# Issuing the activation loads ahead of the weight loads, and the q reload ahead of the x reload

## The chip, the cores and the metric

The kernel runs on the 8 cores of one Trainium2 chip, one core for each of the 8 sequences of the batch. The cores exchange nothing. The metric is the device time of the slowest core, in microseconds.

## The reference

One transformer layer, for x of 8 x 4096 x 1024:

```python
x = x + attn(layernorm(x), w_qkv, w_proj, b_proj)
x = x + ffn(layernorm(x), w1, b1, w2, b2)

def attn(x, ...):                 # 16 heads of 64, linear attention
    q, k, v = split(x @ w_qkv.T)
    q, k = relu(q), relu(k)
    ksum = k.sum(over the sequence)
    z = 1 / (ksum . q + eps)
    context = v k^T               # per head, summed over the whole sequence
    return (context q * z) @ w_proj.T + b_proj

def ffn(x, ...):
    return relu(x @ w1 + b1) @ w2 + b2        # 1024 -> 4096 -> 1024
```

The context sums over the whole sequence, so attention's output needs all of k and v first. The kernel therefore has two stages.

## The kernel before

Activations are held transposed, 1024 channels as 8 chunks of 128 partitions, tokens along the free dimension. TensorE computes in bf16.

**Stage A** (lines 130 to 370) goes over 8 tiles of 512 tokens. For each tile: the load `xa` (f32 in HBM, cast to bf16 by the transfer, 1 MB written, two buffers); VectorE's squares (line 224); TensorE's column sums of x and of its squares against a vector of ones, `emit_statsA` (lines 234 and 239); mean and rstd on VectorE and ScalarE; their broadcast by TensorE (lines 293 and 297); the normalized tile `lnx` on VectorE (lines 307 and 310). Then the q projection (line 277), whose results ScalarE evicts to `qout` (line 285, two buffers) and SP stores to the HBM scratch `qsc` (line 287, 64 stores of 128 KB); then the k and v projection (line 332); then the context (line 184).

The loop is software pipelined and runs from i = 0 to 8. TensorE's program order is: i = 0: statistics of tile 0, broadcast 0, statistics of tile 1. i = 1: Q of tile 0, broadcast 1, K and V of tile 0, context of tile 0, statistics of tile 2. i = 2: Q of tile 1, broadcast 2, and so on. So the statistics of tile i + 1 always stand ahead of Q of tile i. VectorE's order in a step is LayerNorm of tile i, squares of tile i + 1, accumulation of the context of tile i - 1.

The tiles from 2 on are loaded by line 217: in step i GpSimd waits until LayerNorm of tile i - 1 has read its buffer, and issues the load of tile i + 1 into it.

Three engines issue transfers, each on its own queue. GpSimd's queue carries all transfers that cast: `wqkv_sb` (6 MB written, line 164), W1 (8 MB, line 165, in the trace `w_sb`), the projection weights (2 MB, line 166), eight casts of W2 from HBM to HBM as bf16 (`w2bf`, 1 MB each, line 168), and the `xa` tiles (lines 211, 212, 217). All of these but line 217's are issued without a wait, in the order of their lines. SP's queue carries the `qsc` stores.

**Stage B** (line 371 on), behind a barrier of all engines, goes over 16 tiles of 256 tokens: q is reloaded as `qb` (0.5 MB, two buffers), multiplied by the sums of k (`emit_zden`, line 454) and by the context (line 535), scaled by z, projected (line 603), added to the reloaded f32 x (`x1`, 1 MB, two buffers, line 630), normalized, and sent through the two FFN products (lines 673 and 707). W1 is resident, W2 is streamed from `w2bf`. The small table `zsel_sb` is loaded at the start of stage B on GpSimd's queue (line 403) and used by line 551. The first two `x1` and the first two `qb` are issued at lines 465 and 468, by SP, once all `qsc` stores have landed.

Of the kernel before, what the change touches and what calls it, by code (L numbers as in the profile page):

```python
# [18 lines left out]
NB_A = 512  # L19
# [22 lines left out]
def WG(eng, sem, v):  # L42
    if v > 0:
        sem.maxwait = max(sem.maxwait, v)
        eng.wait_ge(sem.h, v)


def build_nc():
    nc = bass.Bass("TRN2", target_bir_lowering=False)
# [14 lines left out]
    xT_r = xT.ap().rearrange("(c p) n -> p c n", p=128)  # L64
# [3 lines left out]
    qsc_r = qsc.ap().rearrange("(c p) n -> p c n", p=128)  # L68
# [3 lines left out]
    with st:  # L72
# [15 lines left out]
        s_xa = [S("s_xa0"), S("s_xa1")]  # L88
# [8 lines left out]
        s_qb = [S(f"s_qb{r}") for r in range(2)]  # L97
# [28 lines left out]
        with ExitStack() as sta:  # L126
# [4 lines left out]
            xa = SA("xa", [128, 2, CK, NB_A], BF16)  # L131
# [29 lines left out]
                kvt[:, :, 1024:2056].rearrange("p s (pr x) -> p s pr x", x=129)[:, :, :, 128:129],  # L161
                1.0))

            s_wq.inc(nc.gpsimd.dma_start(wqkv_sb[:, :, :], wqkvT_r), 16)
            s_w1.inc(nc.gpsimd.dma_start(w1_sb[:, :, :], w1_r), 16)
            s_wp.inc(nc.gpsimd.dma_start(wproj_sb[:, :, :], wprojT_r), 16)
            for d in range(CK):
# [40 lines left out]

            for i in range(NBA + 1):
                if i == 0:  # L210
                    s_xa[0].inc(nc.gpsimd.dma_start(xa[:, 0, :, :], xT_r[:, :, 0:NB_A]), 16)
                    s_xa[1].inc(nc.gpsimd.dma_start(xa[:, 1, :, :], xT_r[:, :, NB_A:2 * NB_A]), 16)
                elif i + 1 < NBA:
                    WG(nc.gpsimd, s_pa1, 8 * i)
                    WG(nc.gpsimd, s_sqp, 8 * i)

                    s_xa[(i + 1) % 2].inc(nc.gpsimd.dma_start(
                        xa[:, (i + 1) % 2, :, :], xT_r[:, :, (i + 1) * NB_A:(i + 2) * NB_A]), 16)
# [154 lines left out]
        with ExitStack() as stb:  # L373
            SBB = lambda name, shape, dt: stb.enter_context(nc.sbuf_tensor(name, shape, dt))
            projtmp = SBB("projtmp", [128, CK, NB_B], F32)
            qb = SBB("qb", [128, 2, CK, NB_B], BF16)
# [30 lines left out]
            NB = NB_B  # L407
# [51 lines left out]
            for b in range(NBB + 1):  # L459
                if b == 0:  # L460
                    s_mz2.inc(nc.scalar.memzero(PB[7][32:33, 0:NB]))
                    WG(nc.sync, s_qst[0], 16 * (4 * NBA))
                    WG(nc.sync, s_qst[1], 16 * (4 * NBA))
                    for t in range(2):
                        s_xb[t].inc(nc.sync.dma_start(
                            x1[:, t, :, :], xT_r[:, :, t * NB:(t + 1) * NB]), 16)
                    for t in range(2):
                        s_qb[t].inc(nc.sync.dma_start(
                            qb[:, t, :, :], qsc_r[:, :, t * NB:(t + 1) * NB]), 16)
                else:  # L470
                    if b + 1 < NBB:
                        t = b + 1
                        WG(nc.sync, s_mmattn, 8 * b)
                        WG(nc.sync, s_qst[0], 16 * 4 * (t // 2 + 1))
                        WG(nc.sync, s_qst[1], 16 * 4 * (t // 2 + 1))
                        s_qb[t % 2].inc(nc.sync.dma_start(
                            qb[:, t % 2, :, :], qsc_r[:, :, t * NB:(t + 1) * NB]), 16)
# [243 lines left out]
                if b >= 1 and b + 1 < NBB:  # L721
                    t = b + 1
# [56 lines left out]
```

How the kernel before makes its waits and increments, by code:

```python
    def inc(self, inst, k=1):  # L36
        inst.then_inc(self.h, k)
        self.n += k
        return self.n
# [2 lines left out]
def WG(eng, sem, v):  # L42
    if v > 0:
        sem.maxwait = max(sem.maxwait, v)
        eng.wait_ge(sem.h, v)
```

## Time and profile before

| | us |
|---|---|
| median of 2 runs | 1875.01 (1869.11 to 1880.91) |
| the profiled execution | 1873.58 |
| its span (slowest core, core 5) | 1872.5 |
| spans of the eight cores | 1852.5 to 1872.5 |
| TensorE busy in the span | 1583.6 (85%) |
| VectorE busy | 603.0 (32%) |
| ScalarE busy | 486.2 (26%) |
| GpSimd busy | 117.5 (6%) |

The profile is of one execution, read on its slowest core; times within it count from the first instruction. The trace has 12000 matmuls. A row of a timeline shows start, duration, engine, line, operation, output and input, count, and in brackets the idle time of the engine before it with what ended it. "SPq" and "POOLq" are the queues on which SP and GpSimd issue transfers; a landing time counts from the issue.

### The profile page before, as it was taken

How to read it: one execution, taken by the hardware profiler on the slowest of the kernel's cores; microseconds unless marked ns; L12 is line 12 of the kernel's file. 1: busy time of each engine (PE TensorE's matmuls, PEld its weight loads, DVE VectorE, ACT ScalarE, POOL GpSimd, SP SyncE). 2: the span in 40 equal slices, each digit the busy share in tenths (PEclk: the TensorE clock that was granted, in tenths of full speed). 3: DMA queues.
4: the chain of work that ended last, by engine and by line, in shares of the span. 5: the costliest groups of instructions: out<-in, count | busy, mean ns of one | idle time of the engine just before them, and what ended most of it. 6: DMA issues, size and time to landing. Idle time of an engine off the chain costs nothing.

```text
span 1872.5 us, 32607 instructions; the slowest of 8 cores (1852.5 to 1872.5 us)
## 1 busy us (share of the span) xinstructions
PE 1583.6 (85%) x12000; PEld 1118.9 (60%) x12000; DVE 603.0 (32%) x1295; ACT 486.2 (26%) x1033; POOL 117.5 (6%) x218
## 2 busy tenths in 40 slices
PE   0000599999999559999999999999999999999998
PEld 0000144344444227887887777877878778788787
DVE  0000433343332154334333342342333433433400
ACT  0000123223323114224133142241331422422421
POOL 1000000000000001101011011010110110110100
PEclk9999799999999869999999999999999999999999
DMA  9999412211200211534534336245343362453353
GB/s 150 163 133 106 61 37 46 46 27 42 46 23 23 67 58 46 194 134 147 188 124 163 126 127 216 96 147 186 121 167 124 120 231 91 147 191 136 135 203 113
DMA packets 90007, 220.25 MB, mean 118 GB/s; under 512 B 4592, under 2 KB 70128, under 8 KB 72192
## 3 DMA queue, kind: packets, MB, share of 16 engines
q0 software_dynamic: 21072, 100.70, 22.4%
q1 hardware_dynamic: 68784, 117.48, 18.4%
q8 instruction: 102, 1.67, 0.4%
q14 instruction: 49, 0.40, 0.1%
HBM read 226.58 MB, written 33.55 MB: 139 GB/s over the span
## 4 chain that ended last, share of the span: by engine, by line
PE 61%; ACT 1%; issue 1%; DVE 1%; DMA 1%; SPq 0%; DVEq 0%; ACTq 0%
PE PB L707 24%; PE PB L673 23%; PE PB L603 7%; PE PB L535 2%; PE PB L551 2%; PE PB L553 1%; PE PB L454 1%; PE PB L512 1%; PE PB L507 1%; ACT hT L683 1%; DMA qb<-qsc 1%; ACT msq L421 0%; ACT PB L649 0%; PE PB L579 0%; DVE zrow L442 0%
## 5 line engine op out<-in xcount | busy, mean ns | idle before, releaser
L673 PE MATMUL PB<-ln,w_sb 128*128 128x256 bf16 x4096 | 459.5, 272 | 9.8 <-ACT hT L683 9.3
L707 PE MATMUL PB<-hT,w2t 128*128 128x256 bf16 x4096 | 449.7, 273 | 2.9 <-ACT hT L683 2.1
L707 PEld LDWEIGHTS PB<-hT,w2t 128*128 128x128 bf16 x4096 | 399.6, 98 | 53.0 <-issue 6.9
L673 PEld LDWEIGHTS PB<-ln,w_sb 128*128 128x128 bf16 x4096 | 370.3, 97 | 93.4 <-issue 17.9
L683 ACT ACTIVATE hT<-PB,b1c_sb 128x256 bf16<-128x256 f32 x512 | 241.4, 474 | 269.5 <-PE PB L673 268.6
L332 PE MATMUL PAkv<-wqkv_sb,lnx 128*128 128x512 bf16 x1024 | 225.2, 382 | 0.0
L715 DVE SCALAR_TENSOR_TENSOR outb<-PB,b2c_sb,x 128x256 f32<-128x256 f32 x128 | 61.9, 483 | 383.9 <-PE PB L707 383.9
L234 PE MATMUL PAst<-xa,ones 128*1 128x512 bf16 x64 | 18.5, 441 | 192.1 <-DMA xa<-xT 192.1
L332 PEld LDWEIGHTS PAkv<-wqkv_sb,lnx 128*128 128x128 bf16 x1024 | 100.3, 99 | 127.1 <-issue 9.5
L565 ACT ACTIVATE zbcs<-PB 128x256 f32<-128x256 f32 x128 | 49.1, 384 | 461.2 <-PE PB L553 453.3
L603 PE MATMUL PB<-attnT,wproj_sb 128*128 128x256 bf16 x1024 | 142.0, 308 | 1.0 <-DVE attnT L571 0.5
L277 PE MATMUL PAq<-lnx,wqkv_sb 128*128 128x512 bf16 x512 | 118.2, 391 | 15.5 <-ACT qout L285 15.5
L603 PEld LDWEIGHTS PB<-attnT,wproj_sb 128*128 128x128 bf16 x1024 | 110.7, 111 | 30.2 <-issue 3.8
L234 PEld LDWEIGHTS PAst<-xa,ones 128*1 128x1 bf16 x64 | 5.3, 91 | 201.9 <-issue 196.6
L277 PEld LDWEIGHTS PAq<-lnx,wqkv_sb 128*128 128x128 bf16 x512 | 50.2, 100 | 82.9 <-issue 29.2
L494 POOL CAST xbf<-x 128x256 bf16<-128x256 f32 x128 | 68.9, 584 | 461.3 <-DVE x L630 461.3
L630 DVE SCALAR_TENSOR_TENSOR x<-projtmp,bprojc_sb,x 128x256 f32<-128x256 f32 x128 | 53.6, 479 | 98.9 <-DMA x<-xT 62.9
L224 DVE TENSOR_TENSOR xsqA<-xa 128x512 bf16<-128x512 bf16 x64 | 22.1, 418 | 189.7 <-DMA xa<-xT 189.7
L307 DVE TENSOR_TENSOR tmpA<-xa,PAq 128x512 f32<-128x512 bf16 x64 | 44.0, 687 | 108.2 <-PE PAq L297 101.9
L259 ACT ACTIVATE msqA<-varA 1x512 f32<-1x512 f32 x8 | 5.0, 628 | 269.3 <-DVE varA L256 269.3
L484 POOL DMA_DIRECT2D w2t<-w2bf x64 | 33.7, 529 | 646.5 <-PE PB L707 646.5
L610 ACT ACTIVATE projtmp<-PB 128x256 f32<-128x256 f32 x128 | 49.2, 384 | 96.5 <-PE PB L603 86.8
(92 smaller groups left out, 925.3 us busy)
## 6 DMA issues: line engine op xcount, KB each, us to landing
w2t<-w2bf SPq DMA_DIRECT2D x64, 1024.0 KB, 7.2
w2t<-w2bf POOLq DMA_DIRECT2D x64, 1024.0 KB, 5.6
x<-xT SPq DMA_DIRECT2D x16, 1024.0 KB, 10.1
outT<-outb SPq DMA_DIRECT2D x16, 1024.0 KB, 5.4
w_sb<-w POOLq DMA_DIRECT2D x1, 8192.0 KB, 92.9
w2bf<-w2r POOLq DMA_DIRECT2D x8, 1024.0 KB, 144.4
xa<-xT POOLq DMA_DIRECT2D x8, 1024.0 KB, 9.0
qsc<-qout SPq DMA_DIRECT2D x64, 128.0 KB, 1.8
```

Source lines behind the costliest of these rows:

```text
L277: q_mm = nc.tensor.matmul(PAq[j % 2][:, 0:NB_A], wqkv_sb[:, c, j * 128:(j + 1) * 128], lnx[:, ii % 2, c, :], start=(c == 0), stop=(c == CK ...
L307: s_pa1.inc(nc.vector.tensor_tensor(tmp[:, :], xa[:, i % 2, c, :], PAq[0][:, 0:NB_A], ALU.mult))
L332: kv_mm = nc.tensor.matmul(PAkv[bank][:, 0:NB_A], lnx[:, ii % 2, c, s * 128:(s + 1) * 128], wqkv_sb[:, c, C + jt * 512:C + (jt + 1) * 512] ...
L494: s_cast2.inc(nc.gpsimd.tensor_copy(xbf2[:, c, :], x1[:, b2 % 2, c, :]))
L565: s_qz.inc(nc.scalar.activation(zbcs[:, p % 2, :], PB[ZBANK[p % 3]][:, 0:NB], AF.Copy))
L603: pj_mm = nc.tensor.matmul(PB[6 + j % 2][:, 0:NB], wproj_sb[:, d, j * 128:(j + 1) * 128], attnT[:, d, :], start=(d == 0), stop=(d == CK - 1))
L610: s_pev.inc(nc.scalar.activation(projtmp[:, j, :], PB[6 + j % 2][:, 0:NB], AF.Copy))
L630: s_x1.inc(nc.vector.scalar_tensor_tensor(x1[:, b2 % 2, k, :], projtmp[:, k, :], bprojc[:, k:k + 1], x1[:, b2 % 2, k, :], ALU.add, ALU.add))
L673: f1_mm = nc.tensor.matmul(PB[w % 2][:, 0:NB], w1_sb[:, c, w * 128:(w + 1) * 128], ln2[:, bb % 2, c, :], start=(c == 0), stop=(c == CK - 1))
L683: s_hev.inc(nc.scalar.activation(hT[:, w, :], PB[w % 2][:, 0:NB], AF.Relu, bias=b1c[:, w:w + 1]))
L707: f2_mm = nc.tensor.matmul(PB[2 + d % 2][:, 0:NB], w2t[:, d % 4, w, :], hT[:, w, :], start=(w == 0), stop=(w == WK - 1))
L715: s_oev.inc(nc.vector.scalar_tensor_tensor(outb[:, d, :], PB[2 + d % 2][:, 0:NB], b2c[:, d:d + 1], x1[:, bb % 2, d, :], ALU.add, ALU.add))
```

## The change

The two first `xa` loads, issued by GpSimd at the head of the loop behind all weight loads, are issued among them: tile 0 ahead of `wqkv_sb`, tile 1 between `wqkv_sb` and W1. At the start of stage B, SP issues the two `qb` loads ahead of the two `x1` loads. No transfer is added or taken away, and no wait is changed.

```diff
@@ -161,7 +161,9 @@
+            s_xa[0].inc(nc.gpsimd.dma_start(xa[:, 0, :, :], xT_r[:, :, 0:NB_A]), 16)
             s_wq.inc(nc.gpsimd.dma_start(wqkv_sb[:, :, :], wqkvT_r), 16)
+            s_xa[1].inc(nc.gpsimd.dma_start(xa[:, 1, :, :], xT_r[:, :, NB_A:2 * NB_A]), 16)
             s_w1.inc(nc.gpsimd.dma_start(w1_sb[:, :, :], w1_r), 16)
             s_wp.inc(nc.gpsimd.dma_start(wproj_sb[:, :, :], wprojT_r), 16)
             for d in range(CK):
@@ -208,8 +210,7 @@
             for i in range(NBA + 1):
                 if i == 0:
-                    s_xa[0].inc(nc.gpsimd.dma_start(xa[:, 0, :, :], xT_r[:, :, 0:NB_A]), 16)
-                    s_xa[1].inc(nc.gpsimd.dma_start(xa[:, 1, :, :], xT_r[:, :, NB_A:2 * NB_A]), 16)
+                    pass
                 elif i + 1 < NBA:
@@ -462,11 +463,11 @@
                     for t in range(2):
+                        s_qb[t].inc(nc.sync.dma_start(
+                            qb[:, t, :, :], qsc_r[:, :, t * NB:(t + 1) * NB]), 16)
+                    for t in range(2):
                         s_xb[t].inc(nc.sync.dma_start(
                             x1[:, t, :, :], xT_r[:, :, t * NB:(t + 1) * NB]), 16)
-                    for t in range(2):
-                        s_qb[t].inc(nc.sync.dma_start(
-                            qb[:, t, :, :], qsc_r[:, :, t * NB:(t + 1) * NB]), 16)
```

## Rows read from the trace of the kernel before

**Rows 1.** The page's 40 slices: TensorE and DMA busy, in tenths of each slice.

```profile
PE   0000599999999559999999999999999999999998
DMA  9999412211200211534534336245343362453353
```

**Rows 2.** Waits until 720 us: engine and line, releaser, total, times, longest.

```profile
PE PAst L234 <- DMA xa<-xT: 192.1, 1, 192.1
...
PE PB L454 <- DMA qb<-qsc: 19.5, 1, 19.5
```

**Rows 3.** Timeline of GpSimd at the start: start, duration, what it issues.

```profile
1.57 1.04 POOL L164 DMA_DIRECT2D wqkv_sb<-wqkvT  x1 [0.87 <-POOLq L49]
2.61 0.89 POOL L165 DMA_DIRECT2D w_sb<-w  x1
...
8.26 0.99 POOL L211 DMA_DIRECT2D xa<-xT  x1
9.18 0.96 POOL L212 DMA_DIRECT2D xa<-xT  x1
```

**Rows 4.** Views of lines 168, 211 and 212, in this order: issue to landing.

```profile
DMA to landing us min/median/max: 113.2/144.4/175.8
...
DMA to landing us min/median/max: 183.7/183.7/183.7
...
DMA to landing us min/median/max: 188.7/188.7/188.7
```

**Rows 5.** DMA view until 198 us: transfer, queue, count, KB each, us to landing.

```profile
w_sb<-w POOLq DMA_DIRECT2D x1, 8192.0 KB, 92.9
...
wqkv_sb<-wqkvT POOLq DMA_DIRECT2D x1, 6144.0 KB, 42.5
```

**Rows 6.** Timeline of TensorE: statistics of tile 0, Q of tiles 0 and 1.

```profile
192.12 2.29 PE L234 MATMUL PAst<-xa,ones 128*1 128x512 bf16 x5 [192.12 <-DMA xa<-xT]
...
195.45 1.91 PE L239 MATMUL PAst<-xsqA,ones 128*1 128x512 bf16 x4
...
222.19 3.63 PE L277 MATMUL PAq<-lnx,wqkv_sb 128*128 128x512 bf16 x16
...
276.25 3.63 PE L277 MATMUL PAq<-lnx,wqkv_sb 128*128 128x512 bf16 x16
282.15 12.21 PE L277 MATMUL PAq<-lnx,wqkv_sb 128*128 128x512 bf16 x48 [2.28 <-ACT qout L285]
```

**Rows 7.** Window: length, busy of PE, PEld, DVE, ACT, POOL, clock, DMA share, GB/s.

```profile
206.00:219.00 13.00, 3.35 (x9) 0.85 (x7) 11.42 (x18) 0.00 (x0) 0.76 (x1) 0.50 0.00 1
```

**Rows 8.** View of line 217, the six later `xa` loads: issue to landing.

```profile
DMA to landing us min/median/max: 8.2/8.4/11.0
```

**Rows 9.** View of line 287, the 64 `qsc` stores: issue to landing.

```profile
DMA to landing us min/median/max: 1.8/1.8/3.9
```

**Rows 10.** The page's queues: SP's, with packets, MB, share of 16 engines.

```profile
q1 hardware_dynamic: 68784, 117.48, 18.4%
```

**Rows 11.** Timeline of the start of stage B.

```profile
643.98 1.01 SPq L465 DMA_DIRECT2D x<-xT  x2
645.04 4.78 SPq L468 DMA_DIRECT2D qb<-qsc  x2
...
654.82 1.86 PE L454 MATMUL PB<-qb,ksmat 128*16 128x256 bf16 x8 [19.54 <-DMA qb<-qsc]
...
667.32 0.36 SPq L476 DMA_DIRECT2D qb<-qsc  x1
...
669.57 0.48 DVE L630 SCALAR_TENSOR_TENSOR x<-projtmp,bprojc_sb,x 128x256 f32<-128x256 f32 x1 [1.76 <-ACT projtmp L610]
```

**Rows 12.** Views of line 465, and of line 476 from 660 to 690 us: landing.

```profile
DMA to landing us min/median/max: 6.3/7.3/8.4
...
DMA to landing us min/median/max: 4.0/4.0/4.0
```

**Rows 13.** DMA view from 630 to 720 us: the `zsel_sb` load.

```profile
zsel_sb<-zsel POOLq DMA_DIRECT2D x1, 32.0 KB, 5.7
```

## The prediction

> **What bounds the kernel now.** I read the page's slices first. TensorE is idle in the first four of the 40 slices and busy in nearly all the others, while the DMA engines are full in just those four [rows 1]. The table of waits then names two long waits of TensorE on a transfer: 192.1 us at line 234, the first statistics of stage A, for the `xa` load; and 19.5 us at line 454, the start of stage B, for the `qb` load [rows 2]. Both are on the path that sets the end, because TensorE is the busy engine behind each of them. The change touches exactly these two places and nothing else.
>
> Why 192 us for a tile of 1 MB: the timeline of the start shows that GpSimd issues `wqkv_sb` at 1.57, `w_sb` (W1) at 2.61, after it the projection weights and the eight `w2bf` casts (lines 166 and 168), and only then, at 8.26 and 9.18, the two `xa` tiles [rows 3]. Their landing times, counted from the issue, are 183.7 and 188.7 us, so they arrive at 192.0 and 197.9 [rows 4]. The landings come in the order of the issues: `wqkv_sb` at 1.6 + 42.5 = 44.1, W1 at 2.6 + 92.9 = 95.5, the `w2bf` casts spread from 113.2 to 175.8 after their issues, then `xa` [rows 3 to 5]. The DMA engines are full all the while [rows 1]. So this queue works first in, first out, at the full rate of the DMA engines, and what matters for a load is what is queued ahead of it.
>
> **Part 1, the order on GpSimd's queue.** No transfer is added or removed. `xa` tile 0 goes ahead of `wqkv_sb`, tile 1 behind it, ahead of W1.
>
> Cost of 1 MB (written) in the full queue: W1 is 8 MB in 95.5 - 44.1 = 51.4 us, 6.4 us each; the second `xa` came 5.9 us after the first. I take 6.0 to 6.2 for an `xa`.
>
> New arrivals: `xa` 0 is first, issued near 1.6, at the 8.4 us (median) of such a load later in the kernel [rows 8]: 10. `wqkv_sb`: 44.1 + 6.2 = 50.3. `xa` 1: 56.5. Tile 0's LayerNorm is long done by then. TensorE's program order is statistics(0), broadcast(0), statistics(1), Q(0), so Q(0) waits for `xa` 1 too. Statistics of a tile that has just landed took from 192.12 to 195.45 + 1.91 = 197.4, 5.2 us [rows 6]. Q(0) therefore starts at 56.5 + 5.2 = 61.7; before, it was 222.19 [rows 6]. Seen there, 160 us are gained. They don't last.
>
> The next thing that is late is tile 2. Its load (line 217) is issued by GpSimd when tile 0's LayerNorm has freed the buffer, at the latest near 10 + 30 = 40 us (from 192.12 to Q(0) at 222.19 was 30) [rows 6]. It joins the same queue, behind W1, the projection weights and all eight casts. And TensorE's order puts statistics(2) ahead of Q(1), so nothing of tile 1 beyond its LayerNorm can be computed until `xa` 2 is there. Tile 0 keeps TensorE from 61.7 for 276.25 - 222.19 = 54.1 us [rows 6], to about 116. Then TensorE stands again.
>
> Arrival of `xa` 2: the queue ahead of it is the same set of transfers as was ahead of the end at 197.9, in another order. One more tile: 197.9 + 6.0 = 203.9. New on these engines is that tile 0's eight `qsc` stores now run inside the full stretch. The hardware queue moved 117.48 MB in 18.4% of the span [rows 10], 344.5 us, 2.9 us per MB; the stores are 1 MB: +3. Take 207, bounds 204 (the stores fit in gaps) and 221. The far bound: the load of 1 MB that ran beside compute landed in 8.2 to 11.0 us [rows 8]; if all loads in the 54 us of tile 0 ran slower by 11.0 / 8.2 = 1.34, the queue loses 54 x (1 - 1/1.34) = 14 us. I choose near the lower end, since a lone load's time includes its own start, which a queue filled well ahead hides.
>
> Q(1) then starts at 207 + 5.2 = 212; before, 276.25. That is 64 us, and from there on the program is the same one. One cost comes with it: TensorE restarts Q(1) straight out of an idle stretch. After the 192 us idle its granted clock was 0.50 (the 1.2 GHz level) from 206 to 219 [rows 7]; only Q(0), 30 us after the first statistics, ran its first 16 matmuls in 3.63 us as Q(1) did [rows 6]. With 16 matmuls of Q(1) at half speed the 3.6 us become about 7, of which the 2.28 us wait behind them, for ScalarE, hides most [rows 6]. I take 2, between 0 (all hidden) and 5 (half speed over twice that stretch). Gain of part 1: 64 - 2 = 62 us, bounds 45 and 67.
>
> Issue costs: 1 us of GpSimd's issue ahead of `wqkv_sb` is inside the 6.2. Tile 3's load (line 217 at the next step) waits for tile 1's LayerNorm only, near 97, so it follows `xa` 2 by 6 us, long before TensorE needs it. W1 lands 12 us later than before, at 108, needed only in stage B; the casts end near 196, needed in stage B too. These are free, by hundreds of microseconds.
>
> Tile 0's Q phase itself will be slower than the 18 us that Q(1) had (276.25 to 282.15 + 12.21) [rows 6]: ScalarE's eviction j waits for the store of j - 2, and a store landed in 1.8 us, in 3.9 at most [rows 9]. It has 207 - 116 = 91 us of slack, so this costs nothing.
>
> **Part 2, the order on SP's queue at stage B.** Before, two `x1` tiles of 1 MB are issued at 643.98, then two `qb` of 0.5 MB at 645.04; TensorE starts line 454 at 654.82 [rows 11]. Now `qb` 0 goes first, at 643.98. The nearest row for a `qb` issued into an idle queue with 2 MB of loads right behind it is the one at 667.32: 4.0 us to landing [rows 11, 12]. So line 454 starts at 648.1: 6.7 us. Bounds: 1 MB of `x1` issued first took 6.3 us [rows 12], so at least 4.4; a 128 KB store's 1.8 [rows 9] would give at most 8.9. The Trainium skill, "DMA: Bandwidth & Descriptors", section "Anatomy of one DMA — SWDGE (gpsimd) path", fits a DMA as 2.0 us plus bytes at 436 GB/s, for the other kind of queue; as an estimate 3.2 us here, by which this gain would be 7.5 instead of 6.7. The row is longer, and the row stands in the sum.
>
> What is late next: `x1` 0, now behind 1 MB of `qb`. It is wanted by VectorE at line 630, 669.57 before [rows 11], about 662.9 after. Two MB from an idle start landed in 8.4 + 0.4 us (`x1` 1) [rows 12], so `x1` 0 is there at 653; 10 us to spare. `zsel_sb`, on GpSimd's queue, landed 5.7 us after its issue, at 650, beside the same 3 MB [rows 13]; it is wanted only after line 454's 1.86 us and VectorE's work on them, past 650. Uncovered, either would cost back at most the 6.7.
>
> **Sum.** 62 + 6.7 = 69 us. Against the profiled execution (1873.58 us, span 1872.5) that is 1804.9; its time is 1.4 below the median of the runs, 1875.01. I predict 1805. By the bounds of the terms the sum is 49 to 76, that is 1798 to 1824.
>
> **The rivals.**
> (a) The gain of the start stays whole: `xa` 2 gets past the queued weights (its own share of the engines) and lands before 116. Then Q(0)'s 160 us hold, with 6.7: 1707. Against it: the first two tiles, issued by 9.2, landed behind everything issued before them [rows 3, 4]. 3%.
> (b) Compute slows the full queue by the far bound, 14 us instead of 3: Q(1) at 221 + 5.2 = 226, 50 us gained, less 2 for the restart, and 6.7: 1873.6 - 54.7 = 1819. For it only the 11.0 us landing [rows 8]. 8%.
> (c) Part 2 gives nothing, because `x1` or `zsel_sb` becomes the wait: 1812. Against it the 10 us of slack. 4%.
> (d) Slower than before: the `qsc` stores starve behind the full load queue. Q(0) holds three store round trips in a row, L each. Tile 0 ends at 61.7 + 3L + 36 (the 54.1 less its Q phase of 18). It reaches `xa` 2 from L = 36. It eats the whole gain when it ends at 276 + 7 = 283, which is L = 62; at L = 75 it ends at 323, 40 us later, and the kernel takes 1914. Against it: L was 3.9 us at most [rows 9]. The Trainium skill, same page, section "Queues, rings and completion order", has each DMA engine take turns between queues at packet granularity, which by itself would keep L within a few packets; the 3.9 us agrees, though no store ran beside a queue this deep. 2%.
> (e) The change does little: the queue before `xa` 2 is stretched by 33 us or more (8 us per MB instead of 6.4 over the 20 MB behind `xa` 1). Then 1838 to 1870. The rates of the queue, 6.4 us per MB for W1, were even. 2%.
>
> **How the numbers follow.** The forecast has 81%. Its own range is 1798 to 1812; before's two runs lie 6 us either side of their median, which widens it to 1793 to 1818. Range with (b) and (c): 1793 to 1821. About 2% (37 us, below 1837.5) is what a measurement of this kernel can tell from no change. Faster by more: the forecast, (a), (b), (c), 96%. Within: 2%. Slower by more: 2%.
>
> **What the profile would show.** Waits: TensorE at line 234 twice, once for about 10 us at the start, once for 80 to 95 us ending near 207, plus a wait for `xa` 1 or `wqkv_sb` ending near 56; Q(0) near 61, Q(1) near 212. Landing of the first line-217 load near 170 us. Line 454 first starts 4 to 5 us after the first `qb` issue. I am wrong if Q(1) starts much before 205 (not first in, first out) or after 225 (queue slowed), or if line 630 waits for `x1` at the first block.

## The result, and the profile after

The changed kernel takes 1808.3 us (median of 11 runs) against 1873.3 before (10 runs). The ratio is 0.965, with a 95% interval of 0.963 to 0.967: 66 us, or 3.5%, faster. (Here and below a few runs, in which one half of the chip ran slower, stand in the medians but not in the ratios; where the two differ, the ratio counts.) The forecast was 1805, with a range of 1793 to 1821. The profiled execution took 1800.57 us, its slowest core is core 0 with a span of 1799.5.

The page's slices of the changed kernel, in tenths, one slice 45 us; they answer to [rows 1]:

```profile
PE   1364299999997599999999999999999999999998
PEclk7667599999999689999999999999999999999999
DMA  9999722112000314352463534634436255363463
```

TensorE now has work in the first slices, but little of it, and at a lower granted clock: of the first four slices, idle before, none is more than six tenths busy, and the fifth holds two tenths. The waits until 660 us (engine and line, releaser, total, times, longest) say why; they answer to [rows 2]:

```profile
PE PAst L235 <- DMA xa<-xT: 108.4, 3, 58.5
...
ACT qout L286 <- DMA qsc<-qout: 44.5, 7, 11.4
...
PE PB L455 <- DMA qb<-qsc: 15.2, 1, 15.2
```

The wait of 192.1 us has become three, together 108.4, the longest 58.5. The wait at stage B went from 19.5 to 15.2. The second row has grown: ScalarE waits for the `qsc` stores, 44.5 us in seven waits, where it was 9.7 us in four before. The timeline of TensorE (start, duration, line; it answers to [rows 6]) puts them in order:

```profile
62.41 2.29 PE L235 MATMUL PAst<-xa,ones 128*1 128x512 bf16 x5 [31.39 <-DMA xa<-xT]
...
66.69 3.63 PE L278 MATMUL PAq<-lnx,wqkv_sb 128*128 128x512 bf16 x16
72.50 5.30 PE L278 MATMUL PAq<-lnx,wqkv_sb 128*128 128x512 bf16 x16 [2.18 <-ACT qout L286]
85.00 3.57 PE L278 MATMUL PAq<-lnx,wqkv_sb 128*128 128x512 bf16 x8 [7.21 <-ACT qout L286]
...
153.20 1.98 PE L186 MATMUL PActx<-kvt 128*128 128x129 bf16 x32 [1.21 <-ACT kvt L348]
213.64 2.29 PE L235 MATMUL PAst<-xa,ones 128*1 128x512 bf16 x5 [58.46 <-DMA xa<-xT]
...
218.82 3.85 PE L278 MATMUL PAq<-lnx,wqkv_sb 128*128 128x512 bf16 x16
224.72 10.52 PE L278 MATMUL PAq<-lnx,wqkv_sb 128*128 128x512 bf16 x48 [2.05 <-ACT qout L286]
```

Q(0) starts at 66.7 instead of 222.2, tile 0 is done at 155, and then TensorE waits 58 us until tile 2 lands at 213.6. Q(1), which was at 276.25 on the slowest core before, is at 218.8. The view of the store line (288) from 60 to 130 us shows how tile 0's eight stores fared beside the full queue (time from issue to landing); before, 3.9 us was the longest [rows 9]:

```profile
DMA to landing us min/median/max: 9.9/15.1/58.2
```

Stage B, which answers to [rows 11]:

```profile
582.52 1.00 SPq L466 DMA_DIRECT2D qb<-qsc  x2
583.58 5.12 SPq L469 DMA_DIRECT2D x<-xT  x2
...
589.02 1.86 PE L455 MATMUL PB<-qb,ksmat 128*16 128x256 bf16 x8 [15.19 <-DMA qb<-qsc]
...
603.77 0.48 DVE L631 SCALAR_TENSOR_TENSOR x<-projtmp,bprojc_sb,x 128x256 f32<-128x256 f32 x1 [1.76 <-ACT projtmp L611]
```

Line 455 starts 6.5 us after SP's first issue instead of 10.8, and line 631 waits for ScalarE as before, not for `x1`.

Where the 66 us are, as a mean over the eight cores' timelines: Q(1) starts at 216.8 (215.2 to 219.0) instead of 273.0 (270.5 to 276.3), 56 us; from the last context product to the first product of stage B 15.9 instead of 21.6 us, 6 us. Together 62. Another 1.6 us lie between Q(1) and the last context product (353.5 instead of 355.1). The rest lies in stage B; neither is in a step that the change touches, and no run explains it.

### The profile page after: what moved, and what is told of

The parts are those of the page before. It is cut to its first block, busy times and chain, and to the rows that moved or that the text cites. A ratio compares the mean times of both kernels' runs of the same rounds, so it can differ in the third digit from the quotient of the medians.

```text
span 1799.5 us, 32607 instructions; the slowest of 8 cores (1786.8 to 1799.5 us)
## 1 busy us (share of the span) xinstructions
PE 1583.6 (88%) x12000; PEld 1116.1 (62%) x12000; DVE 603.3 (34%) x1295; ACT 486.2 (27%) x1033; POOL 117.6 (7%) x218
## 4 chain that ended last, share of the span: by engine, by line
PE 63%; ACT 1%; issue 1%; DVE 1%; DMA 0%; DVEq 0%; ACTq 0%; SPq 0%
PE PB L708 25%; PE PB L674 24%; PE PB L604 7%; PE PB L536 2%; PE PB L552 2%; PE PB L554 1%; PE PB L513 1%; PE PB L455 1%; PE PB L508 1%; ACT hT L684 1%; DMA qb<-qsc 0%; ACT msq L422 0%; ACT PB L650 0%; PE PB L580 0%; DVE zrow L443 0%
## 5 line engine op out<-in xcount | busy, mean ns | idle before, releaser
L278 PE MATMUL PAq<-lnx,wqkv_sb 128*128 128x512 bf16 x512 | 125.5, 407 | 35.3 <-ACT qout L286 35.3
L604 PE MATMUL PB<-attnT,wproj_sb 128*128 128x256 bf16 x1024 | 135.6, 298 | 1.3 <-DVE attnT L572 0.7
L604 PEld LDWEIGHTS PB<-attnT,wproj_sb 128*128 128x128 bf16 x1024 | 106.3, 106 | 28.3 <-issue 4.4
L235 PE MATMUL PAst<-xa,ones 128*1 128x512 bf16 x64 | 19.8, 465 | 108.4 <-DMA xa<-xT 108.4
L619 DVE TENSOR_TENSOR tmp<-x,PB 128x256 f32<-128x256 f32 x128 | 53.9, 421 | 59.0 <-PE PB L586 47.3
L498 DVE TENSOR_TENSOR xsq<-x 128x256 bf16<-128x256 f32 x128 | 65.2, 575 | 2.7 <-DVE x L631 2.6
```

The source lines that it names most:

```text
L278: q_mm = nc.tensor.matmul(PAq[j % 2][:, 0:NB_A], wqkv_sb[:, c, j * 128:(j + 1) * 128], lnx[:, ii % 2, c, :], start=(c == 0), stop=(c == CK ...
L498: s_sq2p.inc(nc.vector.tensor_tensor(xsq2[:, c, :], x1[:, b2 % 2, c, :], x1[:, b2 % 2, c, :], ALU.mult))
L604: pj_mm = nc.tensor.matmul(PB[6 + j % 2][:, 0:NB], wproj_sb[:, d, j * 128:(j + 1) * 128], attnT[:, d, :], start=(d == 0), stop=(d == CK - 1))
L619: s_pa2.inc(nc.vector.tensor_tensor(tmp2[:, :], x1[:, bb % 2, k, :], PB[4][:, 0:NB], ALU.mult))
```

## Experiments

### Each part alone

Part 1 alone puts the two `x1` loads back ahead of `qb`:

```diff
                     for t in range(2):
-                        s_qb[t].inc(nc.sync.dma_start(
-                            qb[:, t, :, :], qsc_r[:, :, t * NB:(t + 1) * NB]), 16)
-                    for t in range(2):
                         s_xb[t].inc(nc.sync.dma_start(
                             x1[:, t, :, :], xT_r[:, :, t * NB:(t + 1) * NB]), 16)
+                    for t in range(2):
+                        s_qb[t].inc(nc.sync.dma_start(
+                            qb[:, t, :, :], qsc_r[:, :, t * NB:(t + 1) * NB]), 16)
```

> Only the first part of the change: the two first activation loads ahead among the weights; stage B issues x1 ahead of qb as before. Theory (the two parts add, and nearly all of the gain is in the first one): the changed kernel's time plus what the qb order gives, 4 to 7 us, so 1812 to 1816; line 454 starts about 10.8 us after SP's first issue of stage B instead of 6.5. Rival (the order in stage B gives nothing, because x1 becomes the wait at the first block): the same time as the changed kernel, about 1808.

Measured: ratio 0.967 (0.965 to 0.970), some 5 us above the changed kernel, the two intervals overlapping. From the last context product to the first product of stage B its cores take 22.6 us, against 15.9.

Part 2 alone is the opposite edit, on the kernel before.

> Only the second part: stage B issues qb ahead of x1, the start of stage A is as before. Theory: 4 to 7 us faster than before, 1866 to 1870, with the first qb landing in 4 to 6.5 us. Rival (x1 or zsel late): no change, 1873.

Measured: ratio 0.994 (0.992 to 0.997), 1868.7 us, 11 us below its own runs of before (7 to 15). Its trace shows the same 15.9 us at that place as the changed kernel has, so 6 us are located and the rest of the 11 isn't. No sign of the rival. The parts add: 0.0326 + 0.0058 is 0.0384 where 0.0351 was measured for both, within their intervals.

### Do the slow stores of tile 0 cost anything?

Six `qout` buffers instead of two (four unused rows of stage A are dropped to make room):

```diff
-            qout = SA("qout", [128, 2, NB_A], BF16)
+            qout = SA("qout", [128, 6, NB_A], BF16)
...
-                        WG(nc.scalar, s_qst[j % 2], 16 * (kq // 2))
+                        WG(nc.scalar, s_qst[kq % 6], 16 * (kq // 6))
```

> The changed kernel with six qout buffers instead of two, so that the eviction of a q block waits for the store of six blocks before. In the changed kernel tile 0's Q phase takes 50 us, because each store takes 10 to 15 us beside the full load queue. Theory (tile 0 has slack, tile 2's load sets Q(1)): tile 0's Q phase falls to 18 to 25 us, the wait for tile 2 grows by as much, Q(1) starts at the same time within 3 us, and the time stays at 1808 within 5. Rival (the slow stores reach the end): the time falls by about 30 us to 1778.

Measured: ratio 0.964 (0.962 to 0.966), the same as the changed kernel's 0.965. Its timeline of TensorE:

```profile
67.62 3.63 PE L274 MATMUL PAq<-lnx,wqkv_sb 128*128 128x512 bf16 x15
73.42 11.99 PE L274 MATMUL PAq<-lnx,wqkv_sb 128*128 128x512 bf16 x47 [2.18 <-ACT qout L282]
...
129.31 1.98 PE L182 MATMUL PActx<-kvt 128*128 128x129 bf16 x32 [1.21 <-ACT kvt L344]
218.06 2.29 PE L231 MATMUL PAst<-xa,ones 128*1 128x512 bf16 x5 [86.77 <-DMA xa<-xT]
```

The Q phase takes 18 us, tile 0 is done 24 us earlier, and the wait for tile 2 grew from 58 to 87 us. The stall was real and cost nothing: tile 2's load is what Q(1) hangs on. On the mean of the cores tile 2 is there at 214.7 us, 3 us later than with two buffers (211.8).

The stores taken out of the full stretch; tile 0's are made up for in the next tile's Q phase (so q of tile 0 is not the reference's). The counts that ScalarE waits for change with it:

```diff
-                        WG(nc.sync, s_qev, 8 * ii + j + 1)
-                        s_qst[j % 2].inc(nc.sync.dma_start(
-                            qsc_r[:, j, ii * NB_A:(ii + 1) * NB_A], qout[:, j % 2, :]), 16)
+                        if ii > 0:
+                            WG(nc.sync, s_qev, 8 * ii + j + 1)
+                            for jj in ([0, 1] if ii == 1 else [ii]):
+                                s_qst[j % 2].inc(nc.sync.dma_start(
+                                    qsc_r[:, j, jj * NB_A:(jj + 1) * NB_A], qout[:, j % 2, :]), 16)
```

> The changed kernel without the eight qsc stores of tile 0 while the loads run: in the next tile's Q phase each block is stored twice, to the columns of tiles 0 and 1, so q of tile 0 is not what the reference has. Same bytes, after the full stretch. Theory (the stores hold the engines 3 us, and everything else in the queue is what it was): tile 2's load lands 3 to 7 us earlier than in the changed kernel (there 210 to 214 over the cores), Q(0) takes 18 us. Rival (TensorE, VectorE and ScalarE at work slow the loads, the stores do not): tile 2 lands at the same time within 1 us, though Q(0) takes 18 us.

Measured in its trace: tile 2 is there at 208.2 us on the mean of the cores (205.6 to 209.7), against 211.8 (210.0 to 214.3) with the stores. On the slowest core:

```profile
67.25 3.87 PE L278 MATMUL PAq<-lnx,wqkv_sb 128*128 128x512 bf16 x16
73.06 10.52 PE L278 MATMUL PAq<-lnx,wqkv_sb 128*128 128x512 bf16 x48 [1.94 <-ACT qout L287]
...
209.56 2.29 PE L235 MATMUL PAst<-xa,ones 128*1 128x512 bf16 x5 [92.02 <-DMA xa<-xT]
```

So the eight stores cost the load queue 3.6 us, where the sum had 3, and the 208 that remain are the queue's own. This price depends on when the stores run: with six buffers, where they run closer together, tile 2 came 6.5 us later than without stores.

### What stands ahead of tile 2

The eight casts issued behind tile 2's load:

```diff
-            for d in range(CK):
+            def emit_cast(d):
                 s_w2pc.inc(nc.gpsimd.dma_start(
                     w2bf.ap()[d * 128:(d + 1) * 128, :, :],
                     w2r_h.ap()[d * 128:(d + 1) * 128, :, :]), 16)
...
                     s_xa[(i + 1) % 2].inc(nc.gpsimd.dma_start(
                         xa[:, (i + 1) % 2, :, :], xT_r[:, :, (i + 1) * NB_A:(i + 2) * NB_A]), 16)
+                    if i == 1:
+                        for d in range(CK):
+                            emit_cast(d)
```

> The changed kernel with the eight w2bf casts issued behind the load of tile 2 instead of ahead of it. Theory (what is queued ahead of tile 2 sets Q(1)): tile 2 lands when the projection weights have, near 140, tile 0 still ends near 153 because of its slow stores, so Q(1) starts near 158 instead of 212 to 219. Now Q(1) runs beside the casts, and its stores are slow too (10 to 15 us each, about 25 us more in the phase): Q(2) near 238 instead of 266 to 271, 30 us gained, 1778. Rival (the wait for tile 2 is not what the path hangs on; the total is set by the engines having to move all 27 MB first): Q(2) stays at 266 to 271 and the time at 1808.

Measured: ratio 0.960 (0.957 to 0.963), 1796.7 us: 10 us gained, not 30. The first half of the theory holds, the second was far too small:

```profile
154.82 3.63 PE L281 MATMUL PAq<-lnx,wqkv_sb 128*128 128x512 bf16 x16
160.73 5.30 PE L281 MATMUL PAq<-lnx,wqkv_sb 128*128 128x512 bf16 x16 [2.28 <-ACT qout L289]
196.61 3.57 PE L281 MATMUL PAq<-lnx,wqkv_sb 128*128 128x512 bf16 x8 [30.58 <-ACT qout L289]
215.64 5.40 PE L281 MATMUL PAq<-lnx,wqkv_sb 128*128 128x512 bf16 x16 [15.46 <-ACT qout L289]
...
260.47 3.63 PE L281 MATMUL PAq<-lnx,wqkv_sb 128*128 128x512 bf16 x16
```

Q(1) starts at 154.8 without a wait for tile 2, so what is queued ahead of it did set Q(1), and it moved by 60 us. But then TensorE stalls for 30.6 and 15.5 us inside Q(1), and Q(2) is at 260.5 where 238 was expected. The view of its store line, for the stores issued from 60 to 100 us (beside W1) and from 150 to 175 (beside the casts):

```profile
DMA to landing us min/median/max: 12.3/14.7/20.0
...
DMA to landing us min/median/max: 35.1/44.4/53.7
```

The second stretch holds only two stores. Beside the casts they took three times as long as those beside W1.

The same with six buffers:

> As the kernel before this one, with six qout buffers. Theory: the stores no longer hold tile 0 (it ends near 129) nor tile 1, so Q(1) starts near 145 when tile 2 has landed, and then tile 3's load, queued behind the casts and landing near 220, is the next wait: Q(2) near 226, 40 to 45 us gained on the changed kernel, about 1766. Rival (two buffers are enough here as they were in the run with six buffers alone): the same time as with two buffers.

Measured: ratio 0.957 (0.954 to 0.960), Q(1) at 146.7, Q(2) at 252.5 instead of 226. 15 us gained on the changed kernel instead of 40 to 45. The theory's next wait, for tile 3, did not come: it landed at 222, as said, while TensorE was in the K and V products. Before them TensorE had stood twice 24 us, at the end of Q(1), for ScalarE, which waited for the stores:

```profile
188.62 2.04 PE L293 MATMUL PAq<-m2A,ones1f 1*128 1x512 f32 x2 [23.79 <-ACT qout L285]
214.88 2.04 PE L297 MATMUL PAq<-varA,ones1f 1*128 1x512 f32 x2 [24.22 <-ACT qout L285]
```

All weights spread over the tiles, two buffers and then six:

```diff
+                    if i == 1:
+                        s_w1.inc(nc.gpsimd.dma_start(w1_sb[:, :, :], w1_r), 16)
+                    elif i == 2:
+                        s_wp.inc(nc.gpsimd.dma_start(wproj_sb[:, :, :], wprojT_r), 16)
+                        for d in range(3):
+                            emit_cast(d)
+                    elif i == 3:
+                        for d in range(3, CK):
+                            emit_cast(d)
```

> The changed kernel with W1 issued behind tile 2, the projection weights and three casts behind tile 3, five casts behind tile 4; two qout buffers. Theory (no activation load waits in the queue any more, but two buffers make every Q phase beside a full queue 20 to 30 us longer): Q(1) near 156, when tile 0 is done, Q(2) near 230, Q(3) near 295 instead of 317 to 324: 1775 to 1782. Rival (the store waits are hidden as before): Q(1) near 118, Q(3) near 225, 1710.

> The same with six qout buffers. Theory: Q(0) at 62 to 67, Q(1) near 130, Q(2) near 186, Q(3) near 240, no wait for an activation tile after the second: 80 to 88 us below the changed kernel, 1720 to 1728. Rival (six buffers can't keep up with 51 us of stores per tile, so that the stores hold each Q phase beside a full queue anyway): 1750 to 1775.

Measured: 0.961 (0.958 to 0.965) with two buffers: Q(1) and Q(2) came as said (160 and 232 on the mean of the cores), Q(3) at 314.7 on the slowest core did not, no better than the casts simply behind tile 2; 0.946 (0.939 to 0.952), 1768.4 us, with six. Its rival's range, not the theory's: with no activation tile late any more (Q(1) at 128.8), Q(2) came only at 206.9 and Q(3) at 278.7. Q(1) and Q(2) still ran beside casts; that this is the cause is what the next runs test.

### Casts and stores kept apart

Six buffers, W1 behind tile 2 and the projection weights behind tile 3 as in the two kernels before, and two casts at a time, each pair issued once a tile's q blocks are done (here the casts' part of the edit):

```diff
                 elif i + 1 < NBA:
+                    if i >= 3:
+                        WG(nc.gpsimd, s_mmkv, 16 * (i - 2) + 1)
+                        emit_cast(2 * (i - 3))
+                        emit_cast(2 * (i - 3) + 1)
                     WG(nc.gpsimd, s_pa1, 8 * i)
```

> Six qout buffers, W1 behind tile 2, the projection weights behind tile 3, and the eight w2bf casts two at a time, each pair issued when a tile's q blocks are done (during its K and V products, tiles 1 to 4), so that casts and qsc stores do not run together. Theory (the casts hold up the stores, 35 to 54 us for one store against 12 to 20 beside W1, and that is what the two spread kernels before this lost): Q phases of all tiles 18 to 25 us, Q(1) near 125 to 130, Q(2) near 180, Q(3) near 233 instead of 279: 45 us below the spread kernel with six buffers, about 1723. Rival (any load beside the stores holds them, W1 as much as the casts; or the casts spill over into the next tile's stores): 1745 to 1768.

Measured: ratio 0.916 (0.912 to 0.920), 1716 us by the ratio (lowest run 1716.0). Its timeline of TensorE, the first row of the Q phases of tiles 1, 2 and 3:

```profile
131.20 3.63 PE L280 MATMUL PAq<-lnx,wqkv_sb 128*128 128x512 bf16 x16
...
184.60 3.63 PE L280 MATMUL PAq<-lnx,wqkv_sb 128*128 128x512 bf16 x16
...
238.03 3.63 PE L280 MATMUL PAq<-lnx,wqkv_sb 128*128 128x512 bf16 x16
```

Every tile from 1 on takes 53 us, as before the change, and the stores issued from 130 to 300 us land in 2.0 us (median). The same bytes move on the same engines; only their timing against the stores differs.

The load of `wqkv_sb` cut in two, its q part ahead of tile 1 and its k and v part behind (TensorE waits for the second part before the first K and V product):

```diff
-            s_wq.inc(nc.gpsimd.dma_start(wqkv_sb[:, :, :], wqkvT_r), 16)
+            s_wq.inc(nc.gpsimd.dma_start(wqkv_sb[:, :, 0:C], wqkvT_r[:, :, 0:C]), 16)
             s_xa[1].inc(nc.gpsimd.dma_start(xa[:, 1, :, :], xT_r[:, :, NB_A:2 * NB_A]), 16)
+            s_wkv.inc(nc.gpsimd.dma_start(wqkv_sb[:, :, C:3 * C], wqkvT_r[:, :, C:3 * C]), 16)
```

> The same with the load of wqkv_sb in two: the q part (2 MB) ahead of tile 1, the k and v part (4 MB) behind it. Theory (Q(0) waits for 10 MB of queue, of which 4 MB are not needed yet): tile 1 lands near 38, Q(0) starts near 44 instead of 62 to 67, and the K and V products find their weights, there at 60 to 65: 18 us below the kernel without the split, about 1705. Rival (LayerNorm of tile 0, done near 43, or the K and V weights are late next): 5 us or less gained.

Measured: 1701.9 us, ratio 0.906 (0.902 to 0.910), 19 us below the kernel without the split, as said. Q(0) is at 45.3 and Q(1) at 99.3:

```profile
45.28 4.56 PE L281 MATMUL PAq<-lnx,wqkv_sb 128*128 128x512 bf16 x16
...
99.33 3.63 PE L281 MATMUL PAq<-lnx,wqkv_sb 128*128 128x512 bf16 x16
```

On the mean of the cores Q(1) came 30 us earlier than without the split (99.7 instead of 129.8), Q(2) only 19 (163.8 instead of 182.6): Q(1) now runs beside W1, and ScalarE waits 10 to 12 us for its stores there. The page's slices:

```profile
PE   2979999999956999999999999999999999999998
DMA  9999644500041353463525446352433626244263
```

This is the fastest of the kernels here, 106 us below the changed one. TensorE is at work from the second slice on, while the DMA engines are full for four slices as before.

The same with two buffers:

> The same as the split kernel with two qout buffers. Theory (a store beside a SBUF load takes 12 to 15 us, and with two buffers that is the pace of Q(0) and Q(1), beside the weights and W1, now without slack): Q(0) takes about 45 to 50 us instead of 20, Q(1) half that more: 35 to 50 us above the kernel with six buffers, 1740 to 1755. Rival (two buffers are enough once the casts are out of the way): within 5 us of it.

Measured: 1731.8 us, ratio 0.922 (0.918 to 0.926), 30 us more; Q(1) is at 138.6 instead of 99.3. The direction is the theory's, the size a little under it: Q(0) took 43 us, about as said, but Q(1) 18, no longer than elsewhere, since W1 had landed by then (at 122). The same buffers that were worth nothing in the changed kernel are worth 30 us here.

### Why the casts hold the stores

The DMA view of the queues (packets, MB, share of 16 engines) in stretches in which stores were under way. First the changed kernel from 67 to 117 us, beside W1; then the casts behind tile 2 with two buffers, from 162 to 195 us:

```profile
q0 software_dynamic: 1317, 7.65, 96.0%
q1 hardware_dynamic: 860, 0.78, 5.9%
```

```profile
q0 software_dynamic: 163, 3.64, 98.8%
q1 hardware_dynamic: 141, 0.13, 1.4%
```

Beside W1 GpSimd's queue passes 1317 packets in 50 us on 16 engines, 0.6 us each; beside the casts 163 in 33 us, 3.2 us each. The stores' queue passes nearly as many packets as the casts' (141 to 163). One store is 128 rows, 8 to an engine: at one row for each turn, 8 x 3.2 = 26 us, 52 for two under way (measured 35 and 54); beside W1 8 x 0.6 x 2 = 10 (measured 12 to 20). This is the Trainium skill's rule that each engine takes turns between its queues packet by packet ("DMA: Bandwidth & Descriptors", section "Queues, rings and completion order"), with a price that the prediction did not put on it. If it is so, shorter packets must help. Each cast cut into four along its rows, on the spread kernel with six buffers:

```diff
+                for w in range(0, WK, 8):
                     s_w2pc.inc(nc.gpsimd.dma_start(
-                        w2bf.ap()[d * 128:(d + 1) * 128, :, :],
-                        w2r_h.ap()[d * 128:(d + 1) * 128, :, :]), 16)
+                        w2bf.ap()[d * 128:(d + 1) * 128, w:w + 8, :],
+                        w2r_h.ap()[d * 128:(d + 1) * 128, w:w + 8, :]), 16)
```

> The spread kernel with six qout buffers (casts beside the stores of tiles 1 and 2), each cast of 1 MB cut into four along its rows: 4 KB of source per row instead of 16 KB. Beside the casts GpSimd's queue moved 163 packets in 33 us on 16 engines, 3.2 us per packet, against 0.6 us beside W1. Theory (an engine takes turns between the queues packet by packet, and the casts' packets are long): packets four times shorter, about 0.8 us, stores landing in 10 to 20 us, Q(1) and Q(2) phases near 20 us instead of 40, Q(3) near 240 instead of 279: about 1730. Rival (it is the writing to HBM on both queues that holds the stores, whatever the packets): Q(1) and Q(2) as without the cut, 1768 within 8.

Measured: 1728.6 us, ratio 0.922 (0.919 to 0.926), against 0.946 uncut: 44 us, with the casts still beside the stores. Q(3) is at 243 on the mean of the cores, against 280 uncut. So the rival, that the writing to HBM holds the stores whatever the packets, fails. The queues from 144 to 163 us:

```profile
q0 software_dynamic: 1018, 1.88, 87.7%
q1 hardware_dynamic: 1016, 0.93, 18.0%
```

1018 packets against 1016: one for one, 0.3 us each. The uncut kernel, six buffers too, in the same stretch:

```profile
q0 software_dynamic: 104, 1.93, 84.5%
q1 hardware_dynamic: 419, 0.38, 6.1%
```

The same megabytes of casts, but 0.38 MB of stores instead of 0.93. The cast packets carried 19 KB each uncut and 1.8 KB cut: ten times less, not four as expected.

This window of the uncut kernel, 104 to 419, is no exception to one for one. Only three casts were in the queue, and towards its end one engine after another runs out of them. From 146 to 156 us, while both queues have work:

```profile
q0 software_dynamic: 50, 1.02, 92.1%
q1 hardware_dynamic: 50, 0.05, 1.7%
```

From 156 to 163 us it is 30 to 345, with the casts' packets taking only 46% of the engines' time. The kernel with all eight casts behind tile 2 and six buffers, from 160 to 180 us:

```profile
q0 software_dynamic: 98, 2.13, 95.5%
q1 hardware_dynamic: 98, 0.10, 1.7%
```

Beside W1 the spread kernel with six buffers has 375 to 374 from 75 to 95 us. So where both queues have work the packets pass one for one, also with six stores under way, and the time of a store follows the length of the other queue's packets.

## Why the prediction was right, and where it missed

**The queue is first in, first out, and tile 2 is what is late next.** Right, and the step that carries the forecast. The first load at line 218 took 170 us from its issue, as said. That Q(0) moves by 156 us and Q(1) only by 56 comes from this alone; moving the casts behind tile 2 moved Q(1) by another 60 us.

**Arrival of tile 2: 207 forecast, 211.8 measured** (mean; 210.0 to 214.3). The stores' term was 3 and is 3.6. The rest is the price of an activation tile at the head of the queue. The sum took 6.0 to 6.2 us, from W1's rate and from the shorter of the two intervals at the queue's end (5.9); the other, from the last cast (183.6) to the first tile (192.0), was 8.4. Measured on the mean of the cores, tile 0 moved `wqkv_sb` from 43.8 to 52.6, and tile 1 landed at 60.1: 16.3 us for the two where 12.4 were put in. These 4 us and the stores' 0.6 are the miss. Tile 0 alone landed at 17, not at 10.

**Gain of part 1: 62 us forecast, 56 measured.** Tile 2 was 5 us later than in the sum, and the 276.25 taken for Q(1) before was the latest of the eight cores, whose mean is 273.0. That is 8 us, of which the 2 put in for the restart come back.

**Restart: 2 us forecast, none seen.** The step "16 matmuls of Q(1) at half speed" did not happen. After the wait of 58 us the granted clock was 0.50 (the 1.2 GHz level) from 213 to 219 us, during the statistics, and 0.97 from 219 to 225: it had risen when Q(1) began. The sixteen matmuls took 3.85 instead of 3.63 us, and the wait for ScalarE behind them 2.05 instead of 2.28, which hid the difference. On core 0 Q(1) to Q(2) is 51.7 us, and was 51.9 before; on the mean of the cores it is 53.0, and was 52.3.

**Tile 0's Q phase: slower, and free.** The verdict held by its slack, the size did not. The prediction went by 3.9 us to a landing; 15.1 is the median, 58.2 the longest, the Q phase took 50 us instead of 18, and of 91 us of slack 58 were left. The row behind the 3.9 was of stores beside one lone load at most; nothing in the trace before had a store beside a deep queue. Rival (d) named this mechanism and its decisive point, 36 us per store. In the changed kernel the stores of tile 0 stay under it but for one of the last two (31.9 and 58.2 us, issued at 116.7 and 119.3, when W1 had landed and the projection weights and the casts came), for which nothing waits; in the kernels that have the casts beside the stores they pass it, and there the time does follow. It was given 2%, and would have deserved the other part of the rule that it quoted: turns are by packet, so the price is set by the length of the other queue's packets.

**Part 2: 6.7 us forecast, 5.8 seen in the traces.** The first `qb` landed in 4.1 to 6.5 us over the cores instead of 4.0. `x1` and `zsel_sb` were not late. The timed runs of this part alone give 11 us (7 to 15), more than the traces explain.

**Sum.** Forecast 62 + 6.7 = 69 against 66 measured. The agreement is in part luck: at the two places that the sum is made of, 62 us were gained, and the other 4 are in no term of it. The mechanism, the order of the waits and the place where TensorE stands again came as forecast.

## What to carry to other kernels

When a start-up stall is a load behind other loads in one queue, work out the arrival of the next load that is needed as well: moving the first tiles forward gains only until the first tile that still stands behind the weights. A step counted at nothing because of slack becomes the bound when the slack goes: two and six store buffers were equal in the changed kernel and 30 us apart in the fastest. And small stores should not share the DMA engines with transfers of long packets; issue those in phases without stores, or cut them.

## What the runs showed of the hardware

A 128 KB store landed in 1.8 us before, where no deep queue stood beside it. With two under way it took 10 to 20 us beside a full queue of W1, and 35 and 54 beside a queue of HBM to HBM casts. With six under way it took 35 to 61 beside the eight uncut casts, which ran out meanwhile, and 10 to 19 beside casts cut in four. The DMA engines were full or nearly so beside each of these loads, so their busy share told nothing of it; the packets of each queue did. While both queues had work, the engines passed one packet of each in turn: 50 to 50 and 98 to 98 beside the casts (2.9 and 3.1 us for each cast packet and engine), 375 to 374 beside W1, 1018 to 1016 beside the cut casts. A ratio over a window in which one queue runs out (104 to 419) hides this.

The first tile, issued first, landed 14 to 17 us after its issue with 25 MB queued behind it, against 8.4 for such a load alone. TensorE then waited for tile 1 in any case, and why it is so was not tested.
